# A Mamba mixer with early expert tiles: output product and router parts placed in other slots, small tables in PSUM, and the up products moved between two sums

## What is computed

```python
n = layernorm(x)
x, z = split(n @ in_proj.T)                   # 1024 channels each
xc = silu(causal_conv4(x))
dt_r, B, C = split(xc @ x_proj.T)             # 128, 16, 16
delta = softplus(dt_r @ dt_proj.T + bias)
h = h * exp(delta * A) + delta * xc * B       # 16 states a channel, along time
y = (sum over the states of h * C + xc * D) * silu(z)
x1 = x + y @ out_proj.T
p = softmax(layernorm(x1) @ gate); the two largest, rescaled to sum 1
out = x1 + sum of both w * (silu(m @ w1) * (m @ w3)) @ w2,   m = layernorm(x1)
```

## Time and profile before

| | us |
|---|---|
| median of 3 runs (4744.27 to 4745.53) | 4744.7 |
| the profiled execution | 4742.25 |
| its span, first to last instruction | 4740.5 |

### The profile page before, as it was taken

One profiled execution on the slowest core, in us unless ns is written; L12 is line 12 of the kernel. 1 busy time (PEld: TensorE's weight loads), 2 busy tenths in 40 slices (PEclk: granted clock), 3 DMA queues, 4 the chain that ended last, 5 costly groups with the idle time before them and its releaser, 6 DMA issues. The chain is left out here.

```text
span 4740.5 us, 70347 instructions
## 1 busy us (share of the span) xinstructions
PE 4202.6 (89%) x25764; PEld 3398.3 (72%) x25764; DVE 2400.2 (51%) x3195; ACT 1954.2 (41%) x4094; POOL 1845.0 (39%) x1416
## 2 busy tenths in 40 slices
PE   5777888888888888888878499999999999999999
PEld 4555667666666766676666388888888888888887
DVE  3999987988888889879889100000000000000000
ACT  6777776776677667767764000000000000000000
POOL 2667766775776677667666100000000000000000
PEclk8788989999999999999998699999999999999999
DMA  3112443444344445434443402103030303012210
GB/s 133 67 36 90 140 147 103 152 151 152 103 160 143 129 135 160 148 103 152 147 134 94 147 14 77 43 16 108 13 106 13 106 16 108 13 52 67 91 30 15
DMA packets 289342, 451.98 MB, mean 95 GB/s; under 512 B 15862, under 2 KB 183414, under 8 KB 280822
## 3 DMA queue, kind: packets, MB, share of 16 engines
q1 hardware_dynamic: 273078, 412.71, 26.7%
q0 software_dynamic: 14768, 34.41, 3.9%
q10 hardware_dynamic: 1296, 2.37, 0.1%
HBM read 920.96 MB, written 45.95 MB: 204 GB/s over the span
## 5 line engine op out<-in xcount | busy, mean ns | idle before, releaser
L546 POOL TENSOR_TENSOR hs<-hs,bc 128x1024 f32<-128x1024 f32 x512 | 1213.2, 2370 | 400.2 <-DVE hs L1108 377.4
L1108 DVE TENSOR_TENSOR_SCAN hs<-dA,pU 128x1024 f32<-128x1024 f32 x512 | 1168.2, 2282 | 24.0 <-ACT dA L651 1.2
L1523 ACT ACTIVATE gate<-pA 128x512 f32<-128x512 f32 x216 | 117.4, 544 | 1861.2 <-PE pB L1565 1861.2
L651 ACT ACTIVATE dA<-delta,aneg 128x255 f32<-128x255 f32 x2048 | 853.4, 507 | 31.7 <-DVE hs L1108 24.7
L1438 POOL DMA_INDIRECT out<-ow,trow x54 | 83.5, 1547 | 1972.5 <-DVE ow L1660 1972.5
L1565 PE MATMUL pA<-xT,w1s 128*128 128x128 f32 x6048 | 800.6, 275 | 0.7 <-ACT xT L1536 0.7
L1565 PE MATMUL pB<-xT,w3s 128*128 128x128 f32 x6048 | 800.1, 275 | 0.0
L966 PE MATMUL pY<-ident,hs 128*128 128x128 f32 x4096 | 558.0, 289 | 267.8 <-POOL hs L546 267.6
L1565 PEld LDWEIGHTS pA<-xT,w1s 128*128 128x128 f32 x6048 | 741.8, 192 | 26.4 <-issue 25.4
L1565 PEld LDWEIGHTS pB<-xT,w3s 128*128 128x128 f32 x6048 | 737.4, 192 | 0.0
L966 PEld LDWEIGHTS pY<-ident,hs 128*128 128x128 f32 x4096 | 491.3, 149 | 338.6 <-POOL hs L546 239.1
(11 more groups left out here) (198 smaller groups left out, 3455.4 us busy)
## 6 DMA issues: line engine op xcount, KB each, us to landing
w1s<-in_w SPq DMA_DIRECT2D x165, 1024.0 KB
w3s<-in_w SPq DMA_DIRECT2D x165, 1024.0 KB
w2s<-in_w SPq DMA_DIRECT2D x165, 1024.0 KB
ew<-in_w SPq DMA_DIRECT2D x273, 512.0 KB, 4.3
win<-in_w_in SPq DMA_DIRECT2D x128, 512.0 KB, 3.8
bc<-bc_d SPq DMA_DIRECT2D x64, 1024.0 KB, 10.0
w1s<-in_w SPq DMA_DIRECT2D x55, 512.0 KB
w3s<-in_w SPq DMA_DIRECT2D x55, 512.0 KB
```

The costliest lines, as they stand in the source:

```text
L546: pool.tensor_tensor(hs[b][:, :, :], hs[b][:, :, :], bc[:, N + g * PN:N + (g + 1) * PN, :], ALU.mult)\
L651: e = act.activation(dA[k % NB][:, i, 1:T], delta[:, c, 1:T], ACT.Exp, scale=aneg[:, c, n:n + 1])
L1108: dve.tensor_tensor_scan(hs[b][:, :, :].rearrange("p n t -> p (n t)"), dA[b][:, :, :].rearrange("p n t -> p (n t)"), pU[:, :, :].rearrange ...
```

## The change

- The output product goes from slots 3 to 6 to slots 1, 2, 4 and 5. Its second tile of tokens goes to pM instead of pS, so it no longer waits for the first `residual`; its first half waits for four gated blocks instead of eight.
- Projection x uses pS for pair 0 and pM for pairs 1 to 3, so each of pairs 2 and 3 waits until the pair before it is read.
- The up products become a function of their own, `expert_up`, called between `sums(u, 0)` and `sums(u, 1)`.
- On DVE `residual` goes to (4, 1) and (6, 3); the variance, the square root and `newton` get about a slot between them; `route` is split into `top`, `share` and `place`, which follow one another from (12, 1). On ACT the square root goes to slot 7 and the router's Exp to slot 13.
- `pick` has its tables in PSUM (etab, eboth, emax, epick); ebase, ekey and eoh stay in SBUF. A copy of the last table is kept for the store at the end.

```diff
+        etab, eboth = small(2 * E, E)[0:1], small(2 * E, E)[0:1]
+        enext = etab[:, 1, :]
+        emax, epick = small(1)[0:1], small(2)[0:1]
-        pO = pS
+        pO = [pS[:, :], pM[:, :, :].rearrange("p h t -> p (h t)")]
-        pX = [pS[:, :].rearrange("p (h t) -> p h t", h=2), pM]
+        pX = [pS[:, :].rearrange("p (h t) -> p h t", h=2), pM, pM, pM]
-        OUT_SLOTS = (3, 4, 5, 6)
+        OUT_SLOTS = (1, 2, 4, 5)
...
-                    if u == 8 and back:
+                    if u == 7 and back:
                         ge(act, var2, r + 1)
...
-                    if u == 12 and back:
+                    if u == 13 and back:
                         ge(act, exp_in, r + 1)
...
-                            ge(pe, taps_in, CH * f + 2 * (u - 1))
+                            ge(pe, taps_in, CH * f + 2 * u)
...
                         t, half = OUT_SLOTS.index(u) // 2, OUT_SLOTS.index(u) % 2
-                        ge(pe, gated, CH * s)
-                        ge(pe, x1_ready, TT * r + t)
+                        ge(pe, gated, CH * s if half else CH * r + CH // 2)
                         ge(pe, rows_ready, r)
                         if front:
-                            ge(pe, taps_in, CH * f + 6)
+                            ge(pe, taps_in, CH * f + (8 if t else 2))
...
                     if u == 9 and front:
                         ge(pe, xc_ready, f + 1)
+                        if back:
+                            ge(pe, x1_ready, TT * r + TT)
...
                     beside(u)
                     if scan:
                         sums(u, 0)
+                    if tile:
+                        expert_up(u)
...
+                        if at == (4, 1):
+                            residual(0)
                         if at == (5, 0):
-                            residual(0)
-                        if at == (6, 0):
                             stats2(0)
+                        if at == (6, 3):
+                            residual(1)
                         if at == (7, 0):
-                            residual(1)
+                            stats2(1)
                         if at == (7, 1):
-                            stats2(1)
-                        if at == (7, 3):
                             aggregate(bk, st2, mv2)
-                        if at == (8, 0):
+                        if at == (7, 2):
                             bk.settle()
                             dve.tensor_scalar(tiny2[0][:, :], mv2[:, :, 1], EPS, None, ALU.add).then_inc(var2, 1)
-                        if at == (8, 1):
+                        if at == (9, 0):
                             ge(dve, sd2, r + 1)
-                            newton(bk, tiny2, 0)
+                        if u == 9:
+                            newton(bk, tiny2, g)
-                        if at == (9, 3):
+                        if at == (10, 0):
                             scales(bk, mv2, tiny2, 1, scale2)
-                        if at == (11, 3):
-                            route(0)
-                        if 12 <= u:
-                            route(4 * (u - 12) + g + 1)
+                        if at == (12, 1):
+                            top(0)
...
+                        if u == 13:
+                            top(5 + 2 * g)
+                            top(6 + 2 * g)
+                        if at == (14, 1):
+                            share(0)
...
+                        if at == (15, 1):
+                            share(7)
+                            place(0)
...
+                        if at == (15, 3):
+                            share(9)
+                            place(2)
...
                 if back:
-                    route(17)
+                    place(3)
```

More of the change, by code:

```diff
@@ L816, in expert, with expert_up @@
                         m.then_inc(e_turned, 1)
+                    if u in DOWN:
+                        for k in range(*DOWN[u]):
+                            i = 2 * ROUNDS + k // PK
+                            if k % PK == 0:
+                                ge(pe, e_out, ROUNDS * jt + ROUNDS)
+                                ge(pe, e_h, ROUNDS * jt + k // PK + 1)
+                                ge(pe, ew_in[i % EW], 16 * (EWLOADS // EW * jt + i // EW + 1))
+                            m = pe.matmul(pE[:, :], ehT[:, k, :], ew[i % EW][:, k % PK * D:(k % PK + 1) * D],
+                                          start=k == 0, stop=k == MK - 1)
+                            if k % PK == PK - 1:
+                                m.then_inc(ew_used, 1)
+                def expert_up(u):
                     if UP0 <= u < UP0 + ROUNDS:
@@ L830, in expert @@
                             m.then_inc(ew_used, 1)
[L831 to L841, removed]
                 def project(ps, rowsT, w, h):
@@ L884, in beside @@
                         for h in range(2):
-                            m = project(pX[u % 2], xnT[1 - odd], win[slot], h)
+                            m = project(pX[u], xnT[1 - odd], win[slot], h)
                         m.then_inc(x_mm, 1)
@@ L1125, in residual @@
                     ge(dve, out_mm, TT * r + t + 1)
-                    dve.tensor_tensor(xb[:, t, 0:D], pO[:, :], xb[:, t, 0:D], ALU.add).then_inc(x1_ready, 1)
+                    dve.tensor_tensor(xb[:, t, 0:D], pO[t], xb[:, t, 0:D], ALU.add).then_inc(x1_ready, 1)
                 def stats2(t):
@@ L1130, in stats2, with top @@
                     bk.done(dve.bn_stats(st2[:, t, :], xb[:, t, 0:D]))
-                def route(i):
+                def top(i):
                     bk.settle()
@@ L1160, in route, with share @@
                         dve.tensor_tensor(sel[:, :, :], ohp[:, :, :], oh[1][:, :, :], ALU.add).then_inc(sel_ready, 1)
-                    if i == 7:
+                def share(i):
+                    bk.settle()
+                    if i == 0:
                         ge(dve, exp_out, r + 1)
                         bk.done(dve.tensor_reduce(r2[:, :], le[:, :, :], AXX, ALU.add))
+                    if i == 1:
+                        bk.done(dve.reciprocal(r2[:, :], r2[:, :]))
+                    if i == 2:
+                        bk.done(dve.tensor_tensor(lep[:, :, :], le[:, :, :], spread(r2), ALU.mult))
+                    if i in (3, 5):
+                        bk.done(dve.tensor_tensor(pw[:, :, :], lep[:, :, :], oh[i // 5][:, :, :], ALU.mult))
+                    if i in (4, 6):
+                        bk.done(dve.tensor_reduce(pk[i // 6][:, :], pw[:, :, :], AXX, ALU.add))
+                    if i == 7:
+                        bk.done(dve.tensor_tensor(r3[:, :], pk[0][:, :], pk[1][:, :], ALU.add))
                     if i == 8:
-                        bk.done(dve.reciprocal(r2[:, :], r2[:, :]))
+                        bk.done(dve.reciprocal(r3[:, :], r3[:, :]))
                     if i == 9:
[L1168 to L1177, removed]
                         ge(dve, scattered, 16 * 2 * TT * r)
@@ new lines, in beside @@
+                        if at == (12, 2):
+                            top(1)
+                            top(2)
+                        if at == (12, 3):
+                            top(3)
+                            top(4)
+                        if u == 13:
[3 more added lines that the diff above has]
+                            share(0)
+                        if at == (14, 2):
+                            share(1)
+                            share(2)
@@ new lines, in beside @@
+                        if at == (14, 3):
+                            share(3)
+                            share(4)
+                        if at == (15, 0):
+                            share(5)
+                            share(6)
+                        if at == (15, 1):
+                            share(7)
+                            place(0)
+                        if at == (15, 2):
+                            share(8)
+                            place(1)
+                        if at == (15, 3):
+                            share(9)
+                            place(2)
```

36 lines of the change are left out of this document (19 added, 17 removed).

## The result

| | before | after |
|---|---|---|
| median of the runs, us | 4744.5 (4743.6 to 4745.5) | 4635.4 (4629.3 to 4638.6) |
| the profiled execution, us | 4742.25 | 4637.9 |
| its span, us | 4740.5 | 4636.1 |
| ratio to before, with its 95% interval | | 0.9768 [0.9752, 0.9785] |

A forecast was written before the change was run, and what follows sets the result against it. DVE, stopped in its strict order by back-part waits of 20.2 us a step, with PE close behind, was taken as the bound. Steps 164 + pick 6 + tail 7 + step 15 7 = 184 us gave 4561 us, range 4495 to 4655.

The forecast's parts named there:

- the returned waits: Mixer's full steps: of 20.2 us of DVE waits removed a step, 6.5 come back waiting for PE's turned blocks.
- inner bounds: Whole time from the terms' own bounds: returned waits 2 to 10 a step, projection x 0 to 6, pick 0 to 26.
- The ranks are asked for a slot earlier, so their 2.4 us go.: Back part, DVE's wait for PE's ranks in step 10: 2.4 us vanish.
- I add 2.2 + 1.6: Slot 7: ACT's silu, root and table load delay its copy of up products; PE's slot 8 ends at 1739.5.
- Projection x ... I take 0.: Slots 2 and 3: ACT's read of each pair hidden by sums and POOL wait; 0, at worst 6 us a step.
- The up products between the sums: PE's up round between two sums: gain up to 2.2 us from ACT's copy, equal to the added wait for POOL.
- The pick: Pick's small DVE operation stops waiting for POOL; 1.7 of 2.2 us moves on, 0.5 a step, 6 us; bounds 0 and 26.
- Tail and step 15: Mixer's end: second output product starts earlier in its own tile, 7 us; step 15 gains half a step's gain, 7 us.
- PE as the bound with its wait for POOL as before: Full steps: POOL may set the pace at the step's beginning; 158.4 us a step, gain 76, 4669 us; chance 0.17.
- Everything goes: Full steps: PE's work shrinks with fewer gaps, no wait returns, DVE is the bound; gain 262, 4483 us; chance 0.11.
- An up round that waits for POOL and makes the kernel slower: Slots 4 to 10: seven rounds wait for POOL, 18.4 us; 176.8 a step, 4909 us in all; chance 0.05.

The follow-up runs named there:

- the second tile: Changed kernel with projection x alternating between two PSUM tiles in the two steps without a back part (-1 and 0): 4624.9 us, ratio 0.9750.
- the last kernel: Changed kernel with root back in slot 8, two projection x tiles in steps without back part, ranks before projection z and down product, `newton` two quarters later: 4595.8 us.
- the ranks first: Changed kernel with root back in slot 8, two projection x tiles in steps without back part, PE's ranks before projection z and down product: 4596.1 us.

## Why the prediction was right and wrong

**What bounds the kernel: right.** The back part's stops were the cost, and moving its operations (the output product earlier, root correction and router later) removed 213.5 us of waiting. As forecast, a part of it came back as a wait of `finish` for PE's turned blocks, which is now the first row. Its size, 5.1 us a step, was forecast as 6.5.

**The number: in the range partly by luck.** The forecast bounded the returned waits at 2 to 10 us a step. The list fell by 9.1 us of the 20.2, so 11.1 came back, more than the bound. The range held since it had been drawn wider, to 4655. Its inner bounds, "about 4510 to 4625", are not what the terms give at their ends, which is 4487 to 4681; the time is above 4625.

**The sum: the mechanism held, the size did not.** A step gained 8.2 us, not 13.7. The missing 5.5 are, by the trace: ranks 3.4, dA 2.5, smaller waits 0.4, DVE's own work and gaps 0.9, less 1.7 by which `finish` grew less than forecast. Three steps of the working failed.

1. "The ranks are asked for a slot earlier, so their 2.4 us go." They went up to 3.4. DVE's read stands in quarter (15, 1) in both kernels; what moved a slot earlier, from (14, 3) to (13, 3), is `sel`, the operand. That could not help: in step 10 before the change PE came to the ranks 4.2 us after `sel` was ready, behind projection z and the down product, and it still stands there. Moving the ranks ahead takes the wait away, though only 11 of 43 us become time, with `softplus` at the step's end waiting next.
2. "I add 2.2 + 1.6", the root in slot 7 charged to PE alone. The same 6.1 us on ACT lie before DVE's dA as well, whose wait falls from 30.8 to 18.1 us with the root in slot 8, and they bring the slow up round; `finish` falls from 61.2 to 20.4. The experiment prices the root's place at 22 us, a third of the 65 us missing in the steps.
3. "Projection x ... I take 0." In full steps PE's list has 4.1 us in all for a read of projection x, in front of the output product. In step -1 there are no sums and no POOL to hide the read, and it cost 9.7 us in this execution (some 4 to 10 over the six with one tile), all given back by the second tile. The bound of 3 us a pair was right; the place was not thought of.

These mends leave some 33 us of the 65: the last kernel gains 131 us in the steps, the forecast was 164. This rest has no single owner that the runs show. `finish` a quarter later, and `newton` two quarters later, each moved their wait to another row with the time unchanged. That fits a pace set in these slots by PE and ACT and not by DVE's order, where a wait taken from DVE is not time; it is argued from the lists of waits, not shown by a run.

**The up products between the sums: neutral alone, not in the changed kernel.** I called the move neutral. Alone it is (+4 us). Together with the rest it is worth some 14 us: PE's wait for the copy of a round is 7.1 us instead of 59.2, and there PE's time seems to count. A term priced on the kernel before was priced in the wrong surroundings.

**The pick: 6 us forecast, nothing found.** I took 1.7 of 2.2 us as moved on, from a pair in step 1. The runs show all of it moving on. The rule of the Trainium skill (SBUF — State Buffer, Who interferes with whom) that a VectorE instruction with two SBUF inputs contends for a port with a GpSimd instruction that reads SBUF would have given nothing beyond the small work between, and the measurement agrees with it, not with my half us.

**Tail and step 15: 14 forecast, 14.0 found.** Divided at the start of the last step's output product (2616.97 us before, 2520.32 after), the step gained 7.3 us and the tail 6.8, so both terms of 7 held. The tail's mechanism shows in PE's timeline: the second product starts as the first ends, against 4 us of gap and a 9.85 us product in the earlier trace rows.

```profile
2520.32 7.54 PE L898 MATMUL pS<-wout,sz 128*128 128x512 f32 x16
2527.70 7.03 PE L898 MATMUL pM<-wout,sz 128*128 128x512 f32 x16
```

**The rivals.** PE as the bound with its wait for POOL as before, 158.4 us a step: the step of 154.8 us lies between it and the forecast's 149.4 (working: 163.1 - 13.7), nearer to this rival, and so does the whole time. Its reason, PE behind POOL, holds in part: that wait fell by a fifth only. Everything goes: not seen, though the clock that it counted on did rise. An up round that waits for POOL and makes the kernel slower: PE's wait for POOL rose by 35 us with that part alone, but it displaced the wait for ACT, and the time moved by 4 us.

## What to carry to other kernels

When operations of one engine are moved to where their inputs are ready, look for each at where its producer stands in the other engine's written order; a result is ready when that engine gets to it, not when its operands are there. When parts are tried alone, try also the whole without each: here the parts added up, and yet three of them overlapped by 14 us that the fourth gave back. Price a stop by the next late result behind it: here 213 us of waits removed gave 99 us of time, and of three single waits taken away afterwards one gave a quarter of itself and two gave nothing that could be told. A cost called hidden needs its cover in every step, the first and the last included.

## What was not expected of the hardware

- The same matmuls in steps 3 to 14 took 1674.5 us before, 1624.9 after and 1616.0 with the ranks first, at granted clocks of 0.93, 0.96 and 0.97. They were shortest, 1608.5 us, with the root alone back in slot 8, which is not the fastest kernel. Shorter waits thus came with some 50 us less of PE's work beside the waits themselves. In one place a round took 5.46 us after a stop, at a mean granted clock of 0.69, and 3.74 without it, so that a part of it ran at 1.2 instead of 2.4 GHz.
- A DVE operation with both inputs in SBUF that meets POOL's product lasts longer, and giving the small one that bore this a PSUM operand did not remove it: that group fell from 24.2 to 1.9 us and the next with both inputs in SBUF rose from 40.6 to 63.9, so that the two together stayed within 1 us of 65.
